# Two batches written out, the projection's heads doubled on ScalarE and normalised on GpSimd, the third query tile's scores in idle banks, and the feed-forward's second product in high and low parts

## The reference

```
x = x + tanh(g_xattn[0]) * perceiver_attention(ctx, layernorm(x), mask)   # 4 heads of 64, queries and further keys from x
x = x + tanh(g_ffn[0])   * spiking_ffn(layernorm(x))                      # h = relu(x W_fc)^2, y = h W_proj, 5 threshold steps
x = x + tanh(g_xattn[1]) * cross_attention(layernorm(x), ctx, ctx)        # 16 heads of 64, 77 keys
x = x + tanh(g_ffn[1])   * routed_ffn(layernorm(x))                       # 8 experts, one per token
```

```
q = ln @ W_q;  kv = concatenate([xn @ W_kv, ln @ W_kv], axis=1)
qn = rmsnorm(q, q_gamma) * SCALE;  kn = rmsnorm(k, k_gamma)
attn = softmax(where(full_mask, qn @ kn^T, neg));  out = (attn @ v) @ W_out + b_out
```

## Time and profile before

| | us |
|---|---|
| median of 3 runs | 996.73 |
| profiled execution | 997.27 |
| its span | 995.5 |
| PE busy | 840.2 (84%), 4566 instructions |
| DVE busy | 597.9 (60%) |
| ACT busy | 377.4 (38%) |
| POOL busy | 200.2 (20%) |

### The profile page before, as it was taken

One profiled execution on the slowest core, in us unless ns is written; L12 is line 12 of the kernel. 1 busy time (PEld: TensorE's weight loads), 2 busy tenths in 40 slices (PEclk: granted clock), 3 DMA queues, 4 the chain that ended last, 5 costly groups with the idle time before them and its releaser, 6 DMA issues.

```text
span 995.5 us, 14990 instructions
## 1 busy us (share of the span) xinstructions
PE 840.2 (84%) x4566; PEld 689.5 (69%) x4567; DVE 597.9 (60%) x1280; ACT 377.4 (38%) x764; POOL 200.2 (20%) x292
## 2 busy tenths in 40 slices
PE   0966999968669999897999979999998119999996
PEld 0545888745448887664788768888886119999996
DVE  4673888855837888693245467899986403333332
ACT  1443676633536667334444303333332003222221
POOL 4440000002500000110001102554554530111111
PEclk9986999998979999998899989999999559999998
DMA  8500000000000000052200037000000254455540
GB/s 223 97 1 1 1 1 1 1 3 0 1 1 1 1 1 1 25 184 66 53 0 0 1 100 240 0 1 1 1 0 1 80 214 161 158 183 182 165 155 8
DMA packets 44753, 57.62 MB, mean 58 GB/s; under 512 B 16505, under 2 KB 35637, under 8 KB 44565
## 3 DMA queue, kind: packets, MB, share of 16 engines
q1 hardware_dynamic: 28339, 49.41, 15.4%
q0 software_dynamic: 2640, 7.30, 2.1%
q10 hardware_dynamic: 13714, 0.19, 1.0%
HBM read 47.06 MB, written 8.21 MB: 56 GB/s over the span
## 4 chain that ended last, share of the span: by engine, by line
PE 52%; issue 24%; DVE 13%; POOL 5%; ACT 2%; DMA 2%; SPq 0%; DVEq 0%; POOLq 0%; ACTq 0%
PE PS L1720 9%; PE PS L1731 8%; PE PS L1011 6%; PE PS L999 5%; PE PS L608 4%; PE PS L1138 4%; PE PS L648 3%; DVE sum L1244 2%; PE PS L1156 2%; POOL rrms L508 2%; DVE mx L1236 2%; PE PS L661 2%; PE PS L1147 2%; PE PS L662 1%; POOL sorted L1586 1%
## 5 line engine op out<-in xcount | busy, mean ns | idle before, releaser
L723 DVE TENSOR_TENSOR PL<-PS,PH 128x512 fp32r<-128x512 f32 x144 | 97.9, 688 | 38.4 <-ACT PH L786 37.9
L786 ACT ACTIVATE PH<-PS 128x512 fp32r<-128x512 f32 x144 | 84.4, 595 | 56.7 <-PE PS L648 55.8
L608 PE MATMUL PS<-KH,QS 128*128 128x512 f32 (+1 forms) x192 | 81.0, 422 | 20.2 <-ACT prob L777 17.8
L777 ACT ACTIVATE prob<-PS,nmax 128x1101 f32<-128x1101 f32 x64 | 75.6, 1181 | 55.7 <-DVE nmax L708 45.9
L648 PE MATMUL PS<-ident,prob 128*128 128x128 f32 (+1 forms) x576 | 92.3, 284 | 4.0 <-DVE PL L723 3.8
L1720 PEld LDWEIGHTS PS<-xeT,w 128*128 128x128 f32 x736 | 88.3, 197 | 3.7 <-issue 1.4
L1720 PE MATMUL PS<-xeT,w 128*128 128x128 f32 x736 | 88.7, 280 | 2.0 <-ACT xeT L1679 2.0
L648 PEld LDWEIGHTS PS<-ident,prob 128*128 128x128 f32 (+1 forms) x576 | 66.8, 143 | 30.5 <-DVE PL L723 18.1
L1731 PE MATMUL PS<-w,hT 128*128 x368 | 83.1, 379 | 0.0
L608 PE MATMUL PS<-KL,QS 128*128 128x512 f32 (+1 forms) x192 | 74.6, 392 | 0.0
L1731 PEld LDWEIGHTS PS<-w,hT 128*128 128x128 f32 x368 | 68.2, 190 | 8.4
(11 more groups left out here) (251 smaller groups left out, 1631.1 us busy)
## 6 DMA issues: line engine op xcount, KB each, us to landing
w<-in_L_ffn_W SPq DMA_DIRECT2D x31, 1024.0 KB, 5.3
xe<-sorted SPq DMA_DIRECT2D x23, 130.0 KB
XR<-in_x SPq DMA_DIRECT2D x4, 512.0 KB, 8.1
sorted<-fill POOLq DMA_DIRECT2D x1, 1560.0 KB, 11.5
sorted<-fill POOLq DMA_DIRECT2D x1, 1430.0 KB, 8.3
vw<-vwn SPq DMA_DIRECT2D x14, 77.0 KB
wk<-in_L_xattn_Wk SPq DMA_DIRECT2D x1, 1024.0 KB, 6.4
wv<-in_L_xattn_Wv SPq DMA_DIRECT2D x1, 1024.0 KB, 9.0
```

Of the source, the lines that this page charges most:

```text
L608: last = pe.matmul(PS[:, bank, c:c + k1 - k0], q, k[:, h, k0:k1], start=k is KH, stop=k is KL and not masked)
L723: dve.tensor_tensor(PL[0:r, at, :], PS[0:r, bank_of(m, j), :], PH[0:r, at, :].bitcast(F32), ALU.subtract) \
L777: act.activation(prob[:, m % 2, s, :], PSf[:, at:at + KEYS], ACT.Exp, bias=nmax[:, m % 2, s:s + 1], accum_out=lsum[:, m % 3, s:s + 1]).the ...
L786: act.activation(PH[0:r, at, :], PS[0:r, bank_of(m, j), :], ACT.Copy).then_inc(tile_high, 1)
```

## The change

The loops over the batches are gone: every engine's two batches are written out, with constants where registers stood. In the projection DVE writes each head once (512 elements), ACT writes the second copy (`qk2_twice`), POOL takes the mean of squares and normalises all groups but the first. The turns of q and of k are counted apart (`heads_turned`, `high_ready`, `low_ready` against `q_part`, `k_part`), each with four turns. The first group of batch 1 is normalised, turned and scaled within batch 0's attention, and its first two q/k products (`AHEAD`) are made there; lnT and sq have memory of their own. In an attention's first round tile 2 of the queries has its scores in banks 5 to 7. In the fold the values of batch 0 come ahead of kw, group 0's turn and split ahead of W_fc, and W_proj is split into high and low. In the feed-forward h is split as well: ACT makes the square twice (`squares`, hTH), DVE the low part (hTL), and PE makes three products (high-high, high-low, low-high) in place of the exact one, each chunk's as soon as it is there. hTL lies on vwn, and DVE waits for all pieces of vw first.

```diff
+    q_part = lambda b, i: (2 * ITEMS - 1) * b + 2 * i + 1
+    k_part = lambda b, i: (2 * ITEMS - 1) * b + 2 * i + (2 if i < LAST else 1)
...
     def dve_project(dve, b):
         item = lambda i: b * ITEMS + i
-        normalize(dve, b, 0)
+        if b == 0:
+            normalize(dve, b, 0)
         for i in range(ITEMS + 2):
             p = i % 2
             if i < ITEMS:
                 dve.wait_ge(sq_ready, item(i) + 1)
                 dve.tensor_reduce(ssum[:, p, :], sq[:, p, :].rearrange("p (h e) -> p h e", e=E0), AX.X, ALU.add) \
                    .then_inc(ssum_ready, 1)
-                dve.wait_ge(ssum_ready, item(i) + 1)
-                dve.tensor_scalar(rms2[:, p, :], ssum[:, p, :], 1.0 / E0, RMS_EPS ** 2, ALU.mult, ALU.max) \
-                   .then_inc(rms_mean, 1)
                 dve.wait_ge(v_high, item(i) + 1)
                 v = PS[:, 5, 0:D].rearrange("p (h e) -> p h e", h=H0)
                 dve.tensor_tensor(VHL[:, i, :, 1, :], v, VHL[:, i, :, 0, :].bitcast(F32), ALU.subtract).then_inc(v_low, 1)
             if i >= 2:
                 j, s = i - 2, (i - 2) % GT
-                dve.wait_ge(high_ready, item(j) + 1)
                 if j < LAST:
+                    dve.wait_ge(high_ready, q_part(b, j))
                     low = QS[E0:P, j // GT, :, s * P:s * P + P]
                     dve.scalar_tensor_tensor(low, PS[E0:P, 6, :].rearrange("p (h n) -> p h n", h=H0), qgam[E0:P, :],
-                                             low.bitcast(F32), ALU.mult, ALU.subtract)
+                                             low.bitcast(F32), ALU.mult, ALU.subtract).then_inc(low_ready, 1)
                 w = P if j < LAST else C + 1
                 cols = slice(j * P, j * P + w)
+                dve.wait_ge(high_ready, k_part(b, j))
...
+                dve.tensor_tensor(qk2[:, p, :, 0, :], rows, rrms[:, p, :].unsqueeze(2).to_broadcast([P, h, E0]), ALU.mult) \
                    .then_inc(qk2_ready, 1)
...
+            if 1 <= i <= ITEMS:
+                act.wait_ge(qk2_ready, item(i))
+                act.activation(qk2[:, 1 - p, :, 1, :], qk2[:, 1 - p, :, 0, :], ACT.Copy).then_inc(qk2_twice, 1)
             if i == 3:
-                scale_rows(1)
+                scale_rows(act, b, 1)
...
+            item = b * ITEMS + i
+            pool.wait_ge(ssum_ready, item + 1)
+            pool.tensor_scalar(rms2[:, p, :], ssum[:, p, :], 1.0 / E0, RMS_EPS ** 2, ALU.mult, ALU.max) \
+                .then_inc(rms_mean, 1)
+            pool.wait_ge(rms_mean, item + 1)
             pool.tensor_tensor(rrms[:, p, :], rms2[:, p, :], minus_half[:, 0:2 * H0], ALU.pow).then_inc(rrms_ready, 1)
+            if i == 0 or i == GT:
+                normalize(pool, b, 1 + i // GT)
...
+        if b + 1 < B:
+            normalize(pool, b + 1, 0)
...
+            pe.wait_ge(qk2_twice, item(i) + 1)
+            if i < LAST:
+                if i >= 1:
+                    pe.wait_ge(low_ready, q_part(b, i - 1))
+                for h in range(H0):
+                    last = turn(h)
+                last.then_inc(heads_turned, 1)
             if i >= 1:
+                pe.wait_ge(low_ready, k_part(b, i - 1))
+            for h in range(H0, 2 * H0):
+                last = turn(h)
+            last.then_inc(heads_turned, 1)
...
+            pe.wait_ge(proj_added, GT * MP * b)
         for i in range(ITEMS + 2):
             if i < ITEMS:
-                qkv(i)
+                if b == 0 or i >= AHEAD:
+                    project_qk(pe, b, i)
+                project_v(pe, b, i)
...
+        def third_scores():
+
+            q = QS[:, 0, 0, 2 * P:2 * P + P]
+            for bank, c, k0, k1 in THIRD_CHUNKS:
+                masked = k1 == KPAD
+                for k in (KH, KL):
+                    last = pe.matmul(PS[:, bank, c:c + k1 - k0], q, k[:, 0, k0:k1], start=k is KH,
+                                     stop=k is KL and not masked)
+            last = pe.matmul(PS[:, 7, 0:C + 1], ones_rows[:], maskr[:, b, :], start=False, stop=True)
+            last.then_inc(third_done, 1)
...
-            if at >= 2:
-                pe.wait_ge(exp_done, GT * MP * b + at - 1)
+            if at >= 3:
+                pe.wait_ge(exp_done, GT * MP * b + (1 if at == 4 else at - 1))
...
+            if m == MP and b + 1 < B:
+                for i in range(AHEAD):
+                    project_qk(pe, b + 1, i)
...
+            if m == MP - 1 and b + 1 < B:
+                turn_rows(pe, b + 1, 0)
...
+            if m == -2:
+                row_max(m + 2, 2)
...
+        pe.wait_ge(fold_read, FOLD_WFC)
+        ffn_turn(pe, 0)
+        bank.narrow(LAST_BANKS)
...
+            own.add(dve.tensor_copy(wprojH[:, c2:c2 + 2, :], turned))
+            own.wait()
+            bank.read(dve.tensor_tensor(wprojL[:, c2:c2 + 2, :], turned, wprojH[:, c2:c2 + 2, :].bitcast(F32), ALU.subtract))
...
-                    for c in range(FC):
-                        last = pe.matmul(PS[:, 4 + half, s * D:s * D + D], hT[:, c, at:at + P], wprojT[:, c, :],
-                                         start=c == 0, stop=c == FC - 1)
+                    products = [(h[:, c, at:at + P], w[:, c, :]) for c in range(FC)
+                                for h, w in ((hTH, wprojH), (hTH, wprojL), (hTL, wprojH))]
+                    for i, (h, w) in enumerate(products):
+                        if half == 0 and s == 0 and i % 3 == 0:
+                            pe.wait_ge(h_ready, FC * g + i // 3 + 1)
+                            pe.wait_ge(h_low, FC * g + i // 3 + 3)
+                        last = pe.matmul(PS[:, 4 + half, s * D:s * D + D], h, w, start=i == 0,
+                                         stop=i == len(products) - 1)
...
+                act.wait_ge(relu_ready, FC * g + c + 1)
+                act.wait_ge(h_low, FC * g + c + 1)
+                act.activation(squares[:, c % 2, :], relu[:, c % 2, :], ACT.Square).then_inc(square_ready, 1)
                 if c == 0:
                     act.wait_ge(y_done, 2 * g + 1)
-                act.wait_ge(relu_ready, FC * g + c + 1)
-                act.activation(hT[:, c, :], relu[:, c % 2, :], ACT.Square).then_inc(h_ready, 1)
+                act.activation(hTH[:, c, :], relu[:, c % 2, :], ACT.Square).then_inc(h_ready, 1)
...
+        def h_lows(g, cs):
+            for c in cs:
+                dve.wait_ge(h_ready, FC * g + c + 1)
+                dve.wait_ge(square_ready, FC * g + c + 1)
+                dve.tensor_tensor(hTL[:, c, :], squares[:, c % 2, :], hTH[:, c, :].bitcast(F32), ALU.subtract) \
+                   .then_inc(h_low, 1)
...
+        for quarter in range(4):
+            dve.wait_ge(vw_moved[quarter], 16 * B * len(pieces_of(quarter)))
         with dve.Fori(0, NG - 1) as g:
+            h_lows(g, range(0, 2))
             dve.wait_ge(g_zT, g + 1)
-            ffn_norm(dve, g + 1)
-            z_low(g + 1)
+            ffn_stats(dve, g + 1)
+            h_lows(g, range(2, 4))
+            ffn_z(dve, g + 1)
+            h_lows(g, range(4, FC))
+            ffn_z_low(dve, g + 1)
```

297 lines of the change are left out of this document (165 added, 132 removed).

## The result

The changed kernel takes 981.94 us (median of 4 runs, 980.31 to 982.38); the kernel before took 997.05 beside it (996.43 to 998.23). The ratio is 0.984, 95% interval 0.983 to 0.986: 15.1 us less. Forecast were 979.0 in a range of 967 to 990.

The account below looks back on a forecast made before the run. TensorE was taken as busy 84% of the span and full in the attention rounds, with time to win in five places outside them. Terms summed to -17.7 us, from 997.27 to 979.6, stated as 979.0; range 967 to 990.

Parts of the forecast that it names:

- seam: Batch 0's last addition to batch 1's first scores: 57.9 us become 40.0 through rows prepared early, -17.9 us.
- third tile: Starts of attention: tile 2's scores in banks 5 to 7 save 2.0 us each (0.5 to 3.5), -4.0 for both.
- fold and feed-forward: Fold gains 0.8, wait for vw costs 10.4 plus 0.9, groups gain 3.0, warmer first group 1.6: +5.9 us.
- tail of batch 0's attention: Rounds 7 and 8 of batch 0: batch 1's early q/k products, scaling and transposes cost +4.0 us.
- Projection, steady items: Projection: TensorE's 3.47 us an item sets the pace, 0.6 us less for each of four to five steady items.
- Projection, start: Projection: fifth item 1.0 us later; GpSimd's 3.7 us normalisation makes VectorE wait about as long as it now spends normalising.
- the loop's turn: Seam: the 4.83 us that VectorE first sits with nothing holding it are the batch loop's turn.
- The wait for vw: Feed-forward's first group: ScalarE's third square waits 10.4 us for the vw pieces, 0.9 more for TensorE's lower clock.
- rival 1: Feed-forward: the wait for vw is short; without it 969 us. Chance 0.12.
- Groups: Feed-forward: with 256-column products at 0.129 us, a group takes 25.9 us, 0.75 less, -3.0 for four.
- Rival 2: Projection: GpSimd becomes the bound, items stay at 4 us and each start waits twice as long: 989 us. Chance 0.17.
- Rival 3: Feed-forward: 256-column products cost 0.214 us, +25.7 in all, 1005 us; slower from 0.187 a product on. Chance 0.04.

Follow-up runs that it names:

- norm_dve: The changed kernel with the second group's and the context's normalisation back on VectorE: 977.03 us, ratio 0.979 to the kernel before.
- before_written: The kernel before with only its loops over the two batches written out on its four engines: 988.58 us, ratio 0.991.
- no_third: The changed kernel with the third query tile's scores of an attention's first round back in banks 0 to 2: 984.67 us, ratio 0.987.
- vwn_apart: The changed kernel with staging tile vwn on used-up cross-attention weights, not sharing memory with hTL; VectorE's wait for vw moved to the cross attention: 970.32 us, ratio 0.973.

## Why the prediction was right, term by term

The direction, the size and the list of places were right. In the two profiled executions four terms were off by two microseconds or more: projection, seam and third tile gained 6.7 us less than forecast, and fold and feed-forward lost 3.3 less. That the sum came out only 2.6 us off is in part luck: the fourth miss made up for half of the other three.

| term | forecast | measured |
|---|---|---|
| projection of batch 0 | -4.2 | -1.95 |
| tail of batch 0's attention | +4.0 | +3.8 |
| seam | -17.9 | -15.45 |
| third tile's scores, both batches | -4.0 | -2.0 |
| registers in the rounds | -1.5 | -1.5 |
| fold and feed-forward | +5.9 | +2.6 |
| all | -17.7 | -15.3 |

(Of the projection's 1.95 us, 0.46 lie ahead of its first product, where nothing was changed; from first product to scores it is 1.5. The tail: from the second last output copy to the last 11.85 instead of 10.47 us, and from the last copy to the last addition's end 6.04 instead of 3.65. Registers: six round periods take 89.04 instead of 89.82 in batch 0 and 89.06 instead of 89.81 in batch 1. Of the 0.8 us that the terms leave, 0.5 lie behind the feed-forward.)

1. **Projection, steady items: right in pace, wrong in number.** An item takes 3.46 us where I forecast 3.47, TensorE at work without a gap, VectorE with slack. But from the fifth item to the ninth it is 14.9 us instead of 16.0, 1.1 less, and I had counted five items at 0.6, 3.0 together. The step behind the fifth item gained only 0.2, and the one to the ninth lost 0.4 (point 3). The tail gained 2.7 where I said 2.2.
2. **Projection, start: a cost wrong, and a wait set to nothing.** I priced GpSimd's normalisation at 0.92 a tile from L1800, which has one scalar a row; with two (mean and root) it takes 1.20 to 1.24, 4.84 for four. The fifth item came 2.3 us late instead of 1.0, in batch 0 and in the seam (15.8 instead of 14.7). norm_dve shows it: the edit costs 2.1 us a batch net, so "about as long as it now spends on normalising" was wrong by that much.
3. **The same scaling again at the ninth item: missed.** I charged the copy ahead of lnT once; the rows show it at the fifth (1.60) and ninth item (0.60), and turning the order round brought 1.5 us a batch.
4. **Seam: right in its parts.** What I called "the loop's turn" was that (before_written). The fifth item came 1.1 late, by point 2. The rest from there, forecast 25.3 (my own terms, 30.0 less 4.9, give 25.1), was 26.7: by points 1 and 3, as the ninth item again took 4.4 us where a steady one takes 3.46.
5. **Third tile: half in these two executions, right at an equal clock.** Stretch and timeline at batch 1's start:

```profile
264.00:275.00 11.00, 6.99 (x26) 5.40 (x25) 5.48 (x8) 5.02 (x8) 0.00 (x0) 0.66 0.00 0
```

```profile
269.07 0.79 PE L666 MATMUL PS<-KH,QS 128*128 128x512 f32 x1 [2.91 <-ACT prob L854]
```

The granted clock is 0.66 there, and tile 3 waits 2.91 us for the same exponential as ever, as I said it would. From first scores to first output copy the clock was 0.77 and 0.82 in the two batches before and 0.68 and 0.73 after. At like clocks the traces give 2 us a batch and a little more (no_third), which is the value that I took; my lower reason ("if TensorE's clock eats it") is what happened to half of it here. Whether the change itself lowers the clock there, no run shows.
6. **Fold: right up to the last tiles.** kc ended 38.9 us after the last addition (forecast 39.0), zTL 44.8 (44.9), W_fc 48.0 (47.8). Then I gave a W_proj tile VectorE's 1.45 us and left out TensorE's four heads behind it: 2.35. The feed-forward started 56.7 after the last addition, not 54.1.
7. **The wait for vw: right, smaller for the reason in 6.** The last piece landed 69.6 us after the last addition (forecast 69.5). Because the group began 2.6 us later, 8.1 us of wait stayed of 10.4; the lower clock behind it cost some 2 us, where I had 0.9, an amount for which I had given no row. vwn_apart took both away and nothing came in their place, so rival 1's 10 us were real, only not to be had in this kernel.
8. **Groups: better than forecast.** 24.8 to 25.3 instead of 25.9. The price of 256 columns was 0.118, not 0.129, which is 0.8 of 75 products; the last low part ended 0.4 earlier in two of the three later groups. The Trainium skill's rule (TensorE: Matmul & The Clock Gate, section "Wait — 56ns, not 53.3ns?") gives 0.109; the measurement lies in the middle between it and my line, and decides.

Rival 2 (GpSimd as the bound of each item) did not happen: VectorE's waits in the steady items are for ScalarE. Its second part, a longer wait at each start, did: 1.1 to 1.3 us each above my term. Rival 3 is out at 0.118 against 0.187.

## What to carry to other kernels

When a buffer is laid on another's memory, ask what still reads the other: one shared staging tile cost 9.4 us here, and the same bytes on dead weights cost nothing. An offload to a slower engine pays only where no short, awaited step stands behind it in that engine's queue. When steps move between engines, add up every engine's work per tile again, TensorE's small products too: the largest sum is the pace.
